# Attention plus mixture of experts on one core: normalized tokens scattered to per-expert regions during routing, expert tiles loaded by SyncE by row number, late weight steps between the first tiles

## What is computed

```python
x = x + attn(layernorm(x))
x = x + moe(layernorm(x))

def attn(h):                       # per head
    q, k, v = relu(h @ Wq), relu(h @ Wk), h @ Wv
    kv = k.T @ v                   # 64x64
    o = (q @ kv) / clip(q @ k.sum(0), 1e-6)
    return concat(o) @ Wo + bo

def moe(h):                        # (2048, 512)
    scores = h @ gate_w.T + gate_b + bias
    s, idx = top_k(scores, 2)
    gates = softmax(s)
    y_e = silu(h @ w1[e].T + b1[e]) @ w2[e].T + b2[e]
    return sum over the two e of gates * y_e
```

## Time and profile before

| what | us |
|---|---|
| median of 3 runs (lowest, highest) | 1015.02 (1014.78, 1015.13) |
| the profiled execution's own time | 1015.14 |
| its span | 1013.4 |
| PE busy | 997.9 (98%) |
| VectorE (DVE) busy | 686.7 (68%) |
| ScalarE (ACT) busy | 513.9 (51%) |
| GpSimd (POOL) busy | 259.8 (26%) |
| granted TensorE clock, mean | 0.999 of full |
| moved by DMA | 75.35 MB, mean 74 GB/s |

### The profile page before, as it was taken

The page is one execution under the profiler, slowest core; times in us unless marked ns, Lnnn a source line. Parts: engine busy times, 40 slices in busy tenths (PEclk is TensorE's granted clock), DMA queues, the critical chain, the costliest instruction groups (busy, mean ns, idle before and its releaser), DMA issues.

```text
span 1013.4 us, 17489 instructions
## 1 busy us (share of the span) xinstructions
PE 997.9 (98%) x5029; PEld 840.2 (83%) x5030; DVE 686.7 (68%) x1552; ACT 513.9 (51%) x1324; POOL 259.8 (26%) x413
## 2 busy tenths in 40 slices
PE   8999999999999999999999999999999989999998
PEld 7788888888888888888788888888888879998996
DVE  6878665565566667757878778787888664544544
ACT  4445544444444456765555555555554953443442
POOL 1000000000000002222433232333333645556564
PEclk9999999999999999999999999999999999999999
DMA  7012500100000011343211111111125635555653
GB/s 261 2 42 84 208 22 21 40 23 21 21 22 21 21 63 63 104 163 114 53 44 50 42 52 41 41 41 41 42 73 143 201 121 98 111 102 98 109 107 48
DMA packets 46861, 75.35 MB, mean 74 GB/s; under 512 B 6089, under 2 KB 18554, under 8 KB 46690
## 3 DMA queue, kind: packets, MB, share of 16 engines
q1 hardware_dynamic: 37010, 56.04, 17.8%
q0 software_dynamic: 9808, 18.79, 10.0%
HBM read 53.14 MB, written 23.50 MB: 76 GB/s over the span
## 4 chain that ended last, share of the span: by engine, by line
PE 89%; DVE 6%; ACT 3%; issue 1%; DMA 1%; POOL 0%; SPq 0%; ACTq 0%; DVEq 0%; POOLq 0%
PE pK L1615 15%; PE pK L1617 15%; PE pK L1616 15%; PE pA L1615 6%; PE pA L1616 6%; PE pA L1617 6%; PE pX L1615 6%; PE pX L1617 5%; PE pX L1616 5%; PE pA L1749 3%; PE pT L1959 2%; PE pT L1695 2%; PE pX L1977 1%; PE pA L1883 1%; DVE w_lo L1524 1%
## 5 line engine op out<-in xcount | busy, mean ns | idle before, releaser
L965 ACT ACTIVATE qs<-q,nrec 128x64 f32<-128x64 f32 x512 | 129.6, 336 | 88.1 <-DVE nrec L1345 85.5
L586 POOL TENSOR_TENSOR wv_lo<-wv_in,wv_hi 128x512 fp32r<-128x512 f32 x4 | 5.2, 1292 | 406.3 <-ACT wo_hi L886 406.3
L1615 PE MATMUL pA<-k_hi,xn_hi 128*128 128x512 f32 x256 | 101.2, 395 | 1.9 <-DVE xn_lo L1199 0.7
L1615 PE MATMUL pK<-wk_hi,xnT_hi 128*128 128x512 f32 (+1 forms) x256 | 100.0, 391 | 0.6 <-DVE xnT_lo L1199 0.6
L1615 PE MATMUL pK<-wq_hi,xnT_hi 128*128 128x512 f32 x256 | 100.4, 392 | 0.0
L1617 PE MATMUL pK<-wq_hi,xnT_lo 128*128 128x512 f32 x256 | 99.9, 390 | 0.0
L1616 PE MATMUL pK<-wk_lo,xnT_hi 128*128 128x512 f32 (+1 forms) x256 | 99.7, 390 | 0.0
L1616 PE MATMUL pA<-k_lo,xn_hi 128*128 128x512 f32 x256 | 99.7, 389 | 0.0
L1617 PE MATMUL pA<-k_hi,xn_lo 128*128 128x512 f32 x256 | 99.7, 389 | 0.0
L1616 PE MATMUL pK<-wq_lo,xnT_hi 128*128 128x512 f32 x256 | 99.7, 389 | 0.0
L1617 PE MATMUL pK<-wk_hi,xnT_lo 128*128 128x512 f32 (+1 forms) x256 | 99.6, 389 | 0.0
(11 more groups left out here) (277 smaller groups left out, 2449.0 us busy)
## 6 DMA issues: line engine op xcount, KB each, us to landing
w_in<-in_ffn_w SPq DMA_DIRECT2D x22, 256.0 KB, 3.9
w_in<-in_ffn_w SPq DMA_DIRECT2D x8, 704.0 KB, 6.4
xn<-in_attn_hidden_states SPq DMA_DIRECT2D x16, 256.0 KB, 6.3
wv_in<-in_attn_Wv SPq DMA_DIRECT2D x16, 256.0 KB, 2.7
wo_in<-in_attn_Wo SPq DMA_DIRECT2D x16, 256.0 KB, 2.9
wk_in<-in_attn_Wq SPq DMA_DIRECT2D x4, 1024.0 KB, 5.4
xnT_dram<-xnT SPq DMA_DIRECT2D x4, 1024.0 KB, 11.6
x_in<-in_attn_hidden_states SPq DMA_DIRECT2D x16, 256.0 KB, 2.6
```

The lines of the kernel that those rows point to most:

```text
L965: i = nc.scalar.activation(qs[:, s], q[:, s], ACT.Copy, scale=nrec[:, b * HC + h:b * HC + h + 1])
L1615: nc.tensor.matmul(dst, lhs[0], rhs[0], start=start, stop=False)
```

## The change

- A DRAM buffer `xr_dram` of 150 tiles of 128 rows takes the place of `xn2_dram`. SyncE fills it with zeros, in ten stores of 15 tiles behind the pair loads of the first half.
- In the routing of each tile POOL scatters the normalized rows themselves to the two slots (`put_rows`), ahead of the two scatters of `meta_dram`. `xn2` has two buffers; SyncE's store of `xn2` is gone. `layernorm2(2)` goes behind `put_slot8(1, 1)`.
- Mask and slots of the last tile move from POOL to VectorE and, with the tables, stand ahead of all of VectorE's `w_lo`. `rank(NT-2)` moves ahead of `subtract_hi(1)`, `rank(NT-1)` ahead of step 8. VectorE computes for each expert tile its row number in `xr_dram` (`rows_of_tiles`).
- SyncE loads each expert tile by that number (`load_rows`); POOL's gathers are gone.
- `PE_STEPS` has 11 steps (13 before). Steps 31 to 45 stand between the products of tiles 0 to 2 and use four banks; the last `w_lo` is waited for ahead of `pe_y(0)`.
- Buffers move to other addresses; some loads of `w1` and `w2` move with them.

```diff
@@ constants
+FILLS = NP - 6
+FROWS = -(-(E * EROWS + NS - T * 2 // P) // FILLS)
+XROWS = FILLS * FROWS
...
-    xn2 = sb("xn2", D, 176 * KB)
+    xn2 = [sb("xn2_0", D, 152 * KB), sb("xn2_1", D, 154 * KB)]
...
+        LATE = 30
...
-        PE_STEPS = [*range(6), 11, 15, 19, 22, 25, 31, 37]
+        PE_STEPS = [*range(8), 14, 18, 23]
@@ sync
             with sp.Fori(1, NP // 2 - 2) as h:
                 for b in range(2):
                     sp.wait_ge(m_put, 2 * h + (b - 1))
                     load_pair(2 * h + b, b)
+                    sp.dma_start(xr_tiles[ds((2 * h + (b - 2)) * FROWS, FROWS)].rearrange("r p n -> p r n"),
+                                 zero[:, :].unsqueeze(1).to_broadcast([P, FROWS, D])).then_inc(s_fill, 16)
...
-                sp.wait_ge(xn2_ready, t)
-                sp.dma_start(xn2_dram[ds((t - 1) * P, P), :], xn2[:, :]).then_inc(xn2_stored, 16)
...
+            def load_rows(i, b):
+                if not (isinstance(i, int) and i < 2):
+                    sp.wait_ge(gT_put, i - 1)
+                row = sp.value_load(tile_row[0:1, ds(i, 1)], min_val=0, max_val=XROWS - 1)
+                sp.dma_start(xg[b][:, :], xr_tiles[ds(row, 1)].rearrange("a p n -> (a p) n")).then_inc(s_t[b], 16)
+
+            sp.wait_ge(tile_row_ready, 1)
             sp.wait_ge(w_put, W1T)
             sp.wait_ge(w_sub_put, W1_SUBS)
-            sp.wait_ge(s_metain, 16)
+            for b in range(2):
+                sp.wait_ge(s_row[b], 16 * NT)
+            load_rows(0, 0)
+            load_rows(1, 1)
+            sp.wait_ge(w_put, W1T + 2 * HB)
             for e in range(6, E):
                 load_w2(e)
+            with sp.Fori(1, NS // 2) as h:
+                for b in range(2):
+                    load_rows(2 * h + b, b)
@@ gpsimd
+            def put_rows(r, b):
+                pool.wait_ge(xn2_ready, r + 1)
+                pool.nop(nofuse=True)
+                for c in range(2):
+                    pool.indirect_dma_start(xr_dram, bass.IndirectOffsetOnAxis(slot_i[b][:, c:c + 1].bitcast(U32), 0),
+                                            xn2[b][:, :], None).then_inc(s_row[b], 16)
                 for c in range(2):
                     pool.indirect_dma_start(meta_dram, ...
...
-            put_mask(NT - 1, 1, 32 * (NT // 2 - 1))
-            put_slots(NT - 1, 1)
+            pool.wait_ge(top_kept, NT)
+            put_vals(NT - 1, 1, 32 * (NT // 2 - 1))
+            pool.wait_ge(last_slots, 1)
+            put_rows(NT - 1, 1)
...
             for i in range(NS):
-                if i + 5 < NS:
-                    gather(i + 5)
                 add_out(i)
@@ scalar
             act_gT(0)
+            w_hi(31)
+            w_hi(32)
+            w_hi(33)
+            act.wait_ge(experts_ready, 1)
+            first_experts = [act.value_load(tile_expert[0:1, i:i + 1], min_val=0, max_val=E - 1) for i in range(2)]
+            act_h(0)
+            act_gT(1)
+            w_hi(34)
+            act.wait_ge(hT_ones, 2)
+            act_silu(0, first_experts[0])
+            w_hi(35)
+            w_hi(36)
+            act_h(1)
+            act_gT(2)
...
@@ vector
+                if k == W1T + 3 * HB + 1:
+                    dve.wait_ge(w_put, W1T + 4 * HB)
...
+            def rows_of_tiles():
+                c = by8(cmp[:, :])
+                dve.wait_ge(up_to_ready, 1)
+                v.tensor_tensor(c, wide(iota_j[:, :], E), many(up_to, TW), ALU.is_ge).then_inc(tiles_step, 1)
+                dve.wait_ge(tiles_step, 6)
+                v.tensor_tensor(c, c, many(spare, TW), ALU.mult).then_inc(tiles_step, 1)
+                dve.wait_ge(tiles_step, 7)
+                dve.wait_ge(last_vals, 1)
+                v.tensor_reduce(row_sum[:, :], c, AX_X, ALU.add).then_inc(tiles_step, 1)
+                dve.wait_ge(tiles_step, 8)
+                v.tensor_tensor(tile_row[:, :], row_sum[:, :], iota_j[:, :], ALU.add).then_inc(tile_row_ready, 1)
...
+            put_scores(NT - 1)
+            put_last_mask()
+            put_slot8(NT - 1, 1)
+            put_last_slots()
+            tiles_per_expert()
+            rows_of_tiles()
+            lo_steps(0, 26)
+            hT_fill()
+            lo_steps(26, 30)
             dve_gT(0)
+            lo_steps(30, 33)
+            dve_gT(1)
+            w_lo(33)
+            dve.wait_ge(experts_ready, 1)
+            dve.wait_ge(s_metain, 16)
+            dve_hT(0, 0)
+            w_lo(34)
+            w_lo(35)
+            dve_gT(2)
+            w_lo(36)
...
+            dve_hT(1, 1)
+            for k in range(37, 41):
                 w_lo(k)
             put_gates()
+            dve_gT(3)
+            for k in range(41, WSTEPS):
+                w_lo(k)
@@ tensor
             subtract_hi(0)
+            rank(NT - 2, 0)
             subtract_hi(1)
...
             pe_gT(0, 0)
+            w_transpose(31)
+            w_transpose(32)
...
             pe_h(0, first_experts[0])
+            w_transpose(33)
             pe_gT(1, 1)
             pe_hT(0)
+            w_transpose(34)
+            w_transpose(35)
+            meta_transpose()
             pe_h(1, first_experts[1])
+            w_transpose(36)
             pe_gT(2, 0)
             pe_hT(1)
+            for k in range(37, 40):
+                w_transpose(k)
+            pe_h(2, first_experts[2])
+            w_transpose(40)
+            pe_gT(3, 1)
+            for k in range(41, WSTEPS):
+                w_transpose(k)
+            pe_hT(2)
+            e = expert(0)
             pe.wait_ge(w_lo_ready, len(DVE_STEPS))
+            pe.wait_ge(far_ready, 1)
+            pe_y(0, 0, e)
+            pe_h(3, expert(3))
+            pe_gT(4, 0)
+            pe_y(1, 1, expert(1))
+            pe_hT(3)
-            with pe.Fori(1, NS // 2) as h:
+            with pe.Fori(2, NS // 2) as h:
```

More of the change, by code:

```diff
@@ L351, in block_kernel @@
         hT_ones = sem("hT_ones")
-        s_g = [sem(f"s_g{i}") for i in range(2)]
+        s_t = [sem(f"s_t{i}") for i in range(2)]
+        s_row = [sem(f"s_row{i}") for i in range(2)]
+        tile_row_ready = sem("tile_row_ready")
+        s_fill = sem("s_fill")
         s_add = [sem(f"s_add{i}") for i in range(2)]
@@ L739, in _ @@
             pool.wait_ge(x2_stored, 16 * NT)
-            pool.wait_ge(xn2_stored, 16 * NT)
+            for b in range(2):
+                pool.wait_ge(s_row[b], 16 * NT)
             pool.wait_ge(dots_done, E * (NT - 2))
@@ L786, in _ @@
             pool.wait_ge(after_ready, 1)
-            for i in range(3, 5):
-                gather(i)
+            pool.wait_ge(ids_ready, 1)
             for i in range(NS):
-                if i + 5 < NS:
-                    gather(i + 5)
                 add_out(i)
@@ L1104, in _ @@
             act.wait_ge(o_put, NC * NT)
-            for k in range(3):
+            for k in range(4):
                 w_hi(k)
@@ L1113, in _ @@
             w_act_lo(2)
+            put_xn2T(1)
             w_hi(5)
             w_act_lo(3)
-            put_xn2T(1)
-            for k in range(6, WSTEPS - 2):
+            w_hi(6)
+            w_act_lo(4)
+            w_hi(7)
+            w_act_lo(5)
+            for k in range(8, 31):
                 w_hi(k)
@@ L1363, in residual, with layernorm2, dots @@
                 nc.vector.tensor_tensor(x2[:, :], o, xb[:, :], ALU.add).then_inc(x2_ready, 1)
-            def layernorm2(t):
+            def layernorm2(t, b):
                 newton_rstd(NT + t)
-                if not (isinstance(t, int) and t == 0):
-                    dve.wait_ge(xn2_stored, 16 * t)
+                if not (isinstance(t, int) and t < 2):
+                    dve.wait_ge(s_row[b], 16 * t - 16 * b)
                     dve.wait_ge(xn2T_put, 1)
-                normalize(xn2[:, :], x2[:, :]).then_inc(xn2_ready, 1)
-            def dots(t, first, last):
+                normalize(xn2[b][:, :], x2[:, :]).then_inc(xn2_ready, 1)
+            def dots(t, b, first, last):
                 dve.wait_ge(xn2_ready, t + 1)
@@ L1515, in _ @@
             dve_qsT(4 * NT - 1, 1)
-            dots(NT - 2, 4, E)
+            dots(NT - 2, 0, 4, E)
             put_scores(NT - 2)
             x2_stats(NT - 1)
-            layernorm2(NT - 1)
+            put_slot8(NT - 2, 0)
+            layernorm2(NT - 1, 1)
             def w_lo(k):
                 dve.wait_ge(w_hi_ready, k + 1)
+                if k == W1T + 3 * HB + 1:
+                    dve.wait_ge(w_put, W1T + 4 * HB)
+                if k == W1T + 2 * HB + 2:
+                    for b in range(2):
+                        dve.wait_ge(s_row[b], 16 * NT)
+                if k == WSTEPS - HB:
+                    dve.wait_ge(w_put, WSTEPS)
                 src, rows, dst = w_step(k, w1_lo, w2_lo, w_bank(k))
@@ L1933, in _ @@
             subtract_hi(5)
-            score(1)
-            for k in range(8, 16):
-                w_transpose(k)
-                if k - 2 in PE_STEPS:
-                    subtract_hi(k - 2)
             rank(NT - 1, 1)
```

256 lines of the change are left out of this document (136 added, 120 removed).

## The result

The changed kernel takes 1022.2 us, median of four executions (1021.0 to 1023.05), the kernel before 1014.9 beside it: a ratio of 1.0069 (95% interval 1.0057 to 1.0081), 7 us or 0.7% slower. Forecast were 1015.7 in a range that ended at 1018.8. In a second comparison the same file took 1024.5 (1024.2 to 1025.1), ratio 1.0092 [1.0077, 1.0108]. The profiled execution took 1022.93, with a span of 1021.2.

The account below looks back on a forecast made before the run. TensorE was taken to bound the kernel, with VectorE the bound in the weight steps. 1015.14 +1.1 (routing start) -0.4 (late steps) = 1015.8, or 1015.7 since that execution is 0.12 above the median; range 1011.6 to 1018.8.

Parts of the forecast that it names:

- Fills: Ten 3.93 MB zero stores behind SyncE's pair loads, about 9.6 us each, hidden in SyncE's waits: cost 0.
- Scatters on POOL, start of routing: Two more row scatters at 1.08 us, 2.76 us of POOL, delay tile 1's mask to 488.5: +1.1 us.
- Rival (b): Slower: row scatters cost POOL 1.95 us like adding ones, delaying masks of tiles 1 and 14: 1019.1 us; chance 0.23.
- the 3.1 us that the prediction sets against the move: Skill's example: VectorE's hold on the shared port stretches a GpSimd DMA from 620 to 3100 ns; some 1024 us in all.
- Scatters, end of routing: Mask of tile 14 delayed to 787.6; TensorE stands from 785.6 to 787.7; VectorE's first w_lo starts at 798.6.
- They land near 802: Tile 15's row scatters, issued by about 800, land near 802, so tile 0's rows don't hold pe_h(0).
- `pe_h(0)` at 811.2: Weight stage, bound by VectorE: the first tile's products start at 811.2, 8.0 us earlier than now.
- Late steps, 5.0 us of holes: Between first tiles, VectorE's 26.2 us plus 5.0 of holes put pe_y(0) at 829.8; gain only 0.4 us.
- Tile loop and tail: SyncE's tile loads come over 9 us ahead against 3.5 us of landing; cost 0, gain 0.

Follow-up runs that it names:

- e: Changed kernel with only token tile 0's four scatters moved behind the mask of tile 1: 1021.6 us.
- r: The changed kernel itself, unaltered, run again in the third set with a second profile: 1024.5 us.
- a: Changed kernel, GpSimd not waiting for row scatters to land ahead of the b2 columns of experts 2 to 5 and the table work: 1023.8 us.
- abp: Changed kernel with the edits of bp and a, and tile 0's buffer over step 14's w1 tile, so SyncE waits for step 14, not 21: 1025.9 us.
- b: Changed kernel with SyncE's w2 loads of experts 3, 4 and 5 issued after the first two tile loads instead of before: 1028.7 us.
- bp: Changed kernel with only the w2 loads of experts 4 and 5 issued after the first two tile loads: 1023.1 us.
- d: Changed kernel with late weight steps 31 to 44 in one piece ahead of pe_h(0) on all three engines: 1022.1 us.
- f: Changed kernel with each of the ten zero fills issued twice, the second into a DRAM tensor nothing reads: 1025.1 us.
- s: Changed kernel with pe_h(3) ahead of pe_y(0) instead of behind it: 1023.9 us.
- t: Changed kernel with 16 unread identity transposes on TensorE while it waits for tile 1's mask: 1022.6 us.
- x: abp with TensorE's expert-number loads ahead of pe_gT(0), ScalarE's ahead of gT_hi(0), step 33 ahead of pe_h(0), later steps one place earlier: 1021.8 us.
- q: x with tile 0/13 scatters, rows_of_tiles later; pe_h(3), step 34, w_lo(30), last tile's row copy, pe_hT(3) earlier: 1016.3 us, ratio 1.0011 against the kernel before.

## Why the prediction was wrong

Against the profiled execution before, +0.7 us was forecast and 7.8 measured: 7.1 too few. They are 1.1 at A, 2.9 for the landing of the last row scatters, 1.8 for `pe_h(0)`, 1.2 for the late steps and 0.1 at the end.

**Fills: right.** Cost 0; doubled, they still cost nothing up to the routing. One fill landed in 12.4 us instead of the 9.6 worked out.

**Scatters on POOL, start of routing: mechanism right, size too small.** Rival (b) falls: the 32 row scatters took 958/1092/1556 ns (min/median/max) against 1080 taken, and the longest are in the steady loop, where GpSimd has slack. Nor does any come near the 3.1 us that the prediction sets against the move; the last tile's second row scatter took 0.96 us with VectorE busy beside it. (That one scatter took 1.45 us and another 0.97 doesn't by itself say that VectorE was the reason, as the prediction has it.) But the loss at A was 2.2, not 1.1. The walk moved the mask by the two scatters, 2.76, to 488.5. It came at 489.4 for two reasons outside the scatters: tile 0's first one started 0.7 us later than before (481.35 against 480.65), and GpSimd's cast of the indices took 0.68 instead of 0.19 us. TensorE takes the mask 0.1 us later. The late start is mostly not the scatters': 0.6 us were gone by the rank of tile 0, which starts between 474.2 and 475.6 in the profiles of these kernels. From that rank to A it is 14.34 us against 12.73, so the scatters cost 1.6, and run e gives all of it back (12.57).

**Scatters, end of routing: right.** TensorE stands 1.44 us before `rank(14)`, 2.1 forecast, and the first `w_lo` of VectorE comes at 800.63, 798.4 on the clock of before; the walk had 798.6. In the eleven other profiles with this order here (r and runs a, abp, b, bp, d, e, f, s, t, x) step 14 comes 1.5 us later behind B: VectorE's slot step for the last tile waits 1.87 to 1.98 us on a releaser that the trace can't name, though TensorE's product for it had started 1.7 us before (797.62 in r). In r ScalarE stands 0.9 us on TensorE's results there too, twice. Why is open.

**"They land near 802": wrong, and worth 2.9 us in one profile, 0 in the next.** Landing was taken from the idle routing loop (2.7 to 3.3 us from 500 to 700 us in the profile after, too), while from 785 to 808 the DMA engines carried weight loads at up to 400 GB/s. The Trainium skill, DMA: Bandwidth & Descriptors, section Queues, rings and completion order, says that a DMA engine takes its queues in turn, a packet at a time, so a scatter would share it with whatever load is under way. The trace agrees in what follows from it, though no row shows the turns themselves: 7.7 to 10.1 us beside the loads (5.7 in r) and under 3.8 us once 1.4 MB of them had been moved away (bp). What hides it in the other profiles is another slip of the walk: step 21, for which SyncE's load waits too, is done at 806.7 in the profile after and 809.5 in r, not at 803.5.

**`pe_h(0)` at 811.2: 3.3 us too early** (33.2 behind B against 36.5 in r, bp and abp). 1.3 are the slot step above. 1.1 are TensorE's three register loads between step 32 and `pe_h(0)`. I had counted ScalarE's two and forgotten TensorE's. The rest is VectorE's steps, 13.4 us to the end of `gT_lo(0)` instead of 12.6. In r the last of the three loads starts at 816.9, behind the end of `gT_lo(0)` at 816.6, and `pe_h(0)` follows at 817.80; in x, where they stand ahead of `pe_gT(0)`, `pe_h(0)` doesn't wait. From the view of `tile_expert` and the timeline of DVE of r:

```profile
L2103 PEldq TENSOR_LOAD <-tile_expert x3: 305/313/495, 815.4 to 816.9; - x3
...
816.03 0.69 DVE L1256 TENSOR_TENSOR gT_lo<-pT,gT_hi 128x512 fp32r<-128x512 f32 x1
```

**Late steps, 5.0 us of holes: 1.2 too few.** The order of the holes was as walked. The one before step 33 took 2.6 instead of 1.3, but most of that excess is the register loads over again, since step 33 stood behind `pe_h(0)`: counted from `pe_h(0)`, step 33's `w_lo` starts after 2.8 us where the walk had 2.5. The rest of the 1.2 is spread (0.75 instead of 0.4 before `hT(0)`, 0.24 before the last three steps, and work a little longer than its sum). So `pe_y(0)` was never to be at 829.8: B to E is 56.3 against the 51.8 forecast, 4.5 more, from small terms missing on three engines that are all near their limit. x took 2.6 of them back by moving one step and the loads, and q's stage is 1.0 us shorter than before. So the stage could gain a little, but not in this order, and no version was faster as a whole.

**The clock: not in the forecast at all.** The change adds pauses of 1.4 to 2.1 us at 489, 789, 818, 822 and 837, and one of 1.36 us between 801 and 805 in the eleven profiles named above. The clock may fall with them, at 1.6 us a time: 5 of 10 times at A, 6 of 11 at the one near 803, 9 of 12 at the 1.81 us ahead of `pe_y(0)`, but 0 of 12 at the 1.44 us near 789. So the length of a pause alone doesn't decide, and the profile first shown has all of them but the one near 803 and not one fall. In r it makes 3.3 of 9.1 us. How much of the spread between executions it explains isn't shown: the one at 1.000 took 1022.93, with the late landing in it. In the kernel before no pause at these places is longer than 0.85 us.

**The account** of r, span 1022.5 against 1013.4: mask of tile 1 1.8, a fall behind it 1.6, B to E 6.1 (a fall 1.7, the slot step 1.3, register loads and steps 1.9, holes 1.2), end -0.3: 9.2, measured 9.1. The profile first shown: mask 2.2, no fall, landing 2.9, slot step -0.2, loads and steps 2.0, holes 1.2, end -0.3: 7.8, as measured.

**Tile loop and tail: right,** -0.3 measured against -0.4, with no gap of TensorE in the loop.

## What to carry over

Walk a stage in which three engines are near their limit to the last instruction, register loads too, or give its end a range of several microseconds upward; here each term forgotten was a loss, none a gain. Take a landing time from a stretch with the traffic that will be there. And price a new pause of TensorE at more than its length, and fill it with the next tile's work where the order allows it. Idle transposes kept the clock up in the one profile that has them; that they gain time isn't shown.
